# Fused transformer block on one core: the last stacking transfers issued ahead of the second rows of maxima in three slots, and one piece of the context loaded in a later slot

## The reference, cut to what matters

```python
shift_a, scale_a, gate_a, shift_m, scale_m, gate_m = split(silu(c) @ W_mod + b_mod, 6)
q, k, v = split(modulate(ln(x), shift_a, scale_a) @ W_qkv + b_qkv)     # 16 heads of 8
x = x + gate_a * (softmax(q k^T * scale) v @ W_proj + b_proj)          # self-attention
q_c = ln(x) @ W_qc + b_qc
k_c, v_c = split(ln(context) @ W_kvc + b_kvc)
x = x + softmax(q_c k_c^T * scale) v_c @ W_cproj + b_cproj             # cross-attention
x = x + gate_m * (gelu(modulate(ln(x), shift_m, scale_m) @ W_mlp1 + b_mlp1) @ W_mlp2 + b_mlp2)
```

## Time and profile before

| what | value |
|---|---|
| three timed runs | 373.79, 377.98, 378.31 us, median 377.98 us |
| profiled execution | 376.56 us |
| its span in the trace | 374.5 us |
| mean granted TensorE clock | 0.986 of full |
| busy share of PE, DVE, ACT, POOL | 91%, 70%, 72%, 56% |
| TensorE clock by fortieth of the span | 9998889999, then 9 throughout |

### The profile page before, as it was taken

How to read it: one execution, slowest core, us unless ns; L and a number is a source line. 1 busy time by engine, 2 the same in 40 slices (tenths; PEclk the granted TensorE clock), 3 DMA queues, 4 the chain that set the end, 5 groups by cost and what they waited for, 6 DMA issues and landing times. The chain is left out here.

```text
span 374.5 us, 16029 instructions
## 1 busy us (share of the span) xinstructions
PE 339.9 (91%) x5888; PEld 231.6 (62%) x5888; DVE 263.8 (70%) x671; ACT 269.8 (72%) x526; POOL 210.0 (56%) x479
## 2 busy tenths in 40 slices
PE   4677877899899999999999999999798999999996
PEld 3455545577676767777677777767665445554444
DVE  6956658698878889887888979888766754443401
ACT  2336465878888887888879888888776756776673
POOL 6862666777767787777877777777455220112100
PEclk9998889999999999999999999999999999999999
DMA  5744552444344444434344344444324200102001
GB/s 131 155 104 129 140 148 59 95 112 104 86 103 106 100 103 97 101 86 111 93 111 112 74 100 114 100 110 96 89 72 98 68 4 3 30 28 56 28 28 56
DMA packets 65788, 33.13 MB, mean 88 GB/s; under 512 B 8471, under 2 KB 65495, under 8 KB 65751
## 3 DMA queue, kind: packets, MB, share of 16 engines
q1 hardware_dynamic: 63847, 32.36, 35.6%
q10 hardware_dynamic: 1904, 0.27, 0.6%
HBM read 4.83 MB, written 2.10 MB: 18 GB/s over the span
## 5 line engine op out<-in xcount | busy, mean ns | idle before, releaser
L862 DVE TENSOR_REDUCE mx<-wide 128x8 f32<-128x1024 f32 x64 | 78.2, 1221 | 26.4 <-PE wide L1347 26.1
L1080 ACT ACTIVATE p_c<-wide 128x1024 f32<-128x1024 f32 x64 | 65.5, 1023 | 21.5 <-PE wide L1358 20.5
L1080 ACT ACTIVATE p_s<-wide 128x1024 f32<-128x1024 f32 x64 | 65.7, 1026 | 12.5 <-PE wide L1358 12.2
L862 DVE TENSOR_REDUCE mxc<-wide 128x8 f32<-128x616 f32 x64 | 50.7, 792 | 4.4 <-PE wide L1347 4.0
L1369 PE MATMUL ps_o<-p_s,v_m 128*32 128x128 f32 x1024 | 42.4, 284 | 0.2
L1369 PE MATMUL ps_o<-p_c,vc_m 128*32 128x128 f32 x1024 | 41.3, 279 | 0.3 <-ACT p_c L1080 0.3
L1347 PE MATMUL wide<-qk_st 62*128 62x128 bf16 x512 | 26.6, 226 | 11.7 <-DMA qk_st<-qkp 6.6
L1347 PEld LDWEIGHTS wide<-qk_st 62*128 62x128 bf16 x512 | 15.2, 97 | 27.9 <-DVE mx L862 13.0
L1410 PE MATMUL wide<-m_nT,w_sb 128*128 128x512 f32 x64 | 30.1, 600 | 0.2 <-DVE mxc L862 0.2
L1369 PEld LDWEIGHTS ps_o<-p_s,v_m 128*32 128x32 f32 x1024 | 25.0, 111 | 7.5 <-issue 1.9
L1369 PEld LDWEIGHTS ps_o<-p_c,vc_m 128*32 128x32 f32 x1024 | 24.1, 109 | 7.0 <-issue 0.5
(11 more groups left out here) (182 smaller groups left out, 822.9 us busy)
## 6 DMA issues: line engine op xcount, KB each, us to landing
qk_st<-qkp SPq DMA_DIRECT2D x94, 128.0 KB, 2.5
qkc_st<-qkcp SPq DMA_DIRECT2D x90, 128.0 KB, 2.5
out<-m_out SPq DMA_DIRECT2D x7, 256.0 KB, 2.3
xs<-x SPq DMA_DIRECT2D x3, 512.0 KB, 5.1
qk_st<-nmT SPq DMA_DIRECT2D x64, 4.0 KB
qkc_st<-nmcT SPq DMA_DIRECT2D x64, 4.0 KB
ctx_sb<-ctx SPq DMA_DIRECT2D x3, 308.0 KB
w_sb<-L_xcond_W_mlp SPq DMA_DIRECT2D x2, 256.0 KB, 3.0
```

What stands on the lines that cost most here:

```text
L862: nc.vector.reduce_max(mxt[:, b].rearrange("q (x r) -> q r x", r=2)[:, r], src, AX.X, negate=True).then_inc(sems[done], 1)
L1080: nc.scalar.activation(dst[u % 2][:].rearrange("k x q -> k (x q)"), ps_st[:].rearrange("k s x -> k (s x)"), ACT.Exp, scale=SCALE).then_inc ...
```

## The change

In SP's `slot`, a function `rest_first` picks slots 0, 1, 2 and 14. In these the last two stacking transfers of the pair ahead are issued before `max_rows` b = 1. For slot 0 that was so already, so slots 1, 2 and 14 change. `load_c(4)` goes from the end of slot 1 to slot 3, between `max_rows` b = 0 and the stacking transfers that wait for `qk1_set`. No other engine's stream changes.

```diff
+        def rest_first(s, a):
+
+            return a.first(4) and not a.first() or s.left() == 0
...
                     max_rows(qk_st[h.par], 0, nmT, f"m_in{h.par}0")
+                if h and h.first(4) and not h.first(3):
+                    load_c(4)
                 if a:
...
-                if a and a.second():
+                if a and rest_first(s, a):
                     w(sp, "qk2_set", a.n + 1)
                     stack(sp, qk_st[a.par], qkp, f"qk_in{a.par}", SELF_ORDER[2])
                 if h:
                     w(sp, "nmT_set", 2 * h.n + 2)
                     max_rows(qk_st[h.par], 1, nmT, f"m_in{h.par}1")
                 if a:
-                    if not a.first(2):
+                    if not a.first() and not rest_first(s, a):
                         w(sp, "qk2_set", a.n + 1)
                         stack(sp, qk_st[a.par], qkp, f"qk_in{a.par}", SELF_ORDER[2])
-                if h and h.second():
-                    load_c(4)
```

## The result

The changed kernel took 386.32 us in the median of six runs (382.43 to 387.42), the kernel before 378.14 in the same comparison (373.79 to 379.42). The ratio is 1.026, with a 95% interval of 1.021 to 1.031. That is a loss of some 10 us where 4 us (380.5 against 376.56) had been forecast; the measured time lies above the range.

A forecast was written before the change was run, and what follows sets the result against it. PE was taken as nearest to full. Terms -0.6 + 0.3 - 1.4 + 3.5 + 1.6 + 0 = +3.4 us on 376.56 gave 380.0, leaned to 380.5; range 378.5 to 382.5, eight times in ten 376.5 to 385.

The forecast's parts named there:

- Which waits go: Starts of slots 2, 3 and 15: PE's stacking waits gone or small, waits for maxima rows at unit 2 instead.
- How long the new waits are: Unit 2 in slots 1, 2 and 14: PE waits 0.83, 1.18 and 0.94 us for the maxima rows.
- The upper value of 1.1 us given for slot 3: Start of slot 3: loss up to 1.1 us if SP's gap of 0.45 us stays in front of the rows.
- The start of slot 2: PE reaches slot 2 sooner: 0.6 us gained, between 0.35 and 0.8.
- The start of slot 3: PE reaches slot 3 later: 0.3 us lost, up to 1.1.
- The clock of slot 2: The clock's fall behind slot 2's front wait does not come: 1.4 us gained, nothing if it comes all the same.
- Slot 15: Start of slot 15: no change, between 0.3 us gained and 0.6 lost.
- The stall: Slot 3: DVE waits 3.7 us for the context load (2.5 to 5.8), so PE's second cross product stalls 3.5.
- The clock behind the stall: Slot 3, behind DVE's stall: the clock falls, costing 1.6 us.
- The sum: Whole kernel: all terms together 3.4 us slower than the profiled 376.56 us, so 380.0; stated as 380.5.

The follow-up runs named there:

- e5: Kernel before with the new order in slot 14 alone, slots 1 and 2 and the context load as before; ratio 0.9993 to the kernel before.
- e3: Changed kernel with DVE's wait for context piece 4 moved to the end of slot 3; ratio 1.0102 to the kernel before, 3.8 us.
- e1: Kernel before with the new order in slots 1, 2 and 14, context load left at the end of slot 1; ratio 1.0088, 3.3 us slower.
- e2: Kernel before with only the context load moved to slot 3, order as before; ratio 1.0079, 3.0 us slower.
- e10: Changed kernel with the old order in slot 14; ratio 1.0198 to the kernel before, 7.5 us slower.
- e9: The changed kernel itself, unchanged, measured again beside the kernel before on one more chip; ratio 1.0268, 10.1 us slower.
- e6: Kernel before with the new order in slots 1 and 2 alone; ratio 1.0051, 1.9 us slower.
- e12: Kernel before with ACT issuing maxima rows b = 1 in slots 1, 2 and 14 and the context load in slot 2; ratio 0.9941, 2.2 us faster.
- e15: Kernel before with ACT issuing maxima rows b = 1 in slots 1 and 2 and the context load in slot 3; ratio 1.0061, 2.3 us slower.
- e8: Changed kernel with the context load ahead of the first stacking transfer of pair 4 in slot 3; ratio 1.0131 to the kernel before, 4.9 us.
- e14: Changed kernel with the new order kept in slot 2 only; ratio 1.0143 to the kernel before, 5.4 us slower.
- e4: Kernel before with the context load in slot 2, order as before; ratio 0.9989 to the kernel before.

## Why the prediction was wrong, step by step

- **Which waits go.** Right: all three waits for stacking transfers in slots 2, 3 and 15 went in the changed kernel's trace, and waits of unit 2 for `qk_st<-nmT` came in their place, as the prediction had it.
- **How long the new waits are.** Too small. Predicted 0.83, 1.18 and 0.94 us; measured 1.52, 2.46 and 1.59. In slot 1, PE reached unit 2 0.4 us sooner than before (47.68) and the rows took 2.37 us, not the 2.24 of the earlier trace rows. In slot 2 the rows were issued 4.40 us after the first of the five stacking transfers (65.08 less 60.68), not 2.59 and 1.31 (63.97 less 61.38, and the swap): SP's issue of the third took 1.72 us, where it had taken 1.25 before and the others take 0.6. The issue of the rows took 1.57 us, and they landed after 2.92 us. One quiet landing in slot 0 was too little to price a landing behind five stacking transfers. The upper value of 1.1 us given for slot 3 does not follow from the gap of 0.45 us that it names (0.26 and 0.45 are 0.7).
- **The start of slot 2.** Predicted 0.6 us gained, a term that failed: slot 1 became 0.5 us longer over all traces. The gain rested on the removal of a wait of 1.64 us, and that wait was one draw. It stood in three of five traces of the old order, where slot 1 took 16.3 to 16.7 us; in the other two it was 0.44 and 0.43 us, and slot 1 took 15.3 and 15.0. The eight traces of the new order lie between and above, at 15.8 to 17.1.
- **The start of slot 3.** Predicted 0.3 us lost, and this is a term that failed: with the new order slot 2 is 2.3 us longer over all traces. The wait itself grew by 1.5 us (2.46 less the 0.92 that it replaces), and the clock falls behind it, which I had not counted there.
- **The clock of slot 2.** Predicted 1.4 us gained; another term that failed. The fall that I read in the earlier trace rows is not a feature of the order. With the same order up to there, slot 2 was 17.54 us in one trace and 15.38 in another (e5). I took one draw for a cost that could be removed. In the changed kernel the clock fell sooner, behind slot 1's wait. The net gain of 1.7 us put on slots 1 and 2 (0.6, less 0.3, and 1.4) became a loss of 0.5 us in slot 1 and 2.3 in slot 2.
- **Slot 15.** Predicted nothing; 0.7 us over the traces, not resolved in time by itself (e5).
- **The stall.** Right in mechanism and size: 4.0 us on DVE and 3.88 on PE, predicted 3.7 and 3.5, inside 2.5 to 5.8. e3, with the wait moved, shows that it is the wait. The fit of the Trainium skill (DMA: Bandwidth & Descriptors, "Anatomy of one DMA — SWDGE (gpsimd) path") would have made it too short: it is stated for transfers that GpSimd issues, its 2.7 us are an estimate, and this load, issued by SP, landed after 3.6 to 5.9 us.
- **The clock behind the stall.** Predicted 1.6 us. In the changed kernel's own trace it was 6 us at half clock, and slot 3 grew by 6.2 us in all, 2.3 us more than PE's wait. Over eight traces slot 3 grew by 4.3 us, and PE's wait was 3.4 in the mean (3.2 to 3.9), so 0.9 is left for the clock. So 1.6 us was too much as a mean and too little for this trace; the spread is what I lacked.
- **The sum.** The forecast of 3.4 us was -1.7 for the order and 5.1 for the load. Measured alone: +3.3 and +3.0. The order has the wrong sign, and that is 5.0 us of error; the load alone was overrated by 2.1 us. Of the 6.7 us missed (10.1 less 3.4) these make 2.9. The rest, 3.8 us (10.1 less 3.3 and 3.0), is in neither part alone. The three intervals together leave this some 3 us uncertain.

**What stays open.** The last 3.8 us. By the lengths of slots there is less of it: the new order's 0.5, 2.3 and 0.7 us make 3.5, about e1's 3.3, but the load makes slot 3 4.3 us longer, where e2's time grew by only 3.0 (1.5 to 4.4). With the load, slot 3 is 20.7 us long behind a slot 2 of the new order (five traces) and 20.2 otherwise (three).

The clock looks like an answer and is not shown to be one. The mean granted clock of the runs was 0.982 to 0.986 for the kernel before, 0.979 for e1, 0.986 for e2, and 0.966 and 0.955 for the changed kernel (0.959 for e10). But this mean is no measure of time lost. Call 1 less the granted clock, times the length of a stretch, its missing clock. In e9's trace 17 us are missing over the whole span, and 9.8 of them lie before slot 1. There the clock is at half from 18 us on, and PE is busy hardly longer than in the kernel before. One window of each (the kernel before, then e9):

```profile
18.00:33.00 15.00, 10.06 (x111) 6.87 (x111) 9.98 (x22) 7.05 (x13) 8.54 (x19) 0.99 0.41 94
```

```profile
18.00:33.00 15.00, 10.28 (x109) 7.15 (x109) 10.60 (x22) 6.70 (x13) 8.21 (x19) 0.50 0.41 93
```

Slot 1 begins on the ruler at 36.1 us in e9 and at 35.3 to 36.4 in the kernel before, e2, e5 and e6, which had full clock there or nearly. The trace of e12, the fastest of all, is at half clock in that window too. And of the runs of the kernel before that enter the ratios of e1 to e15, 48 had a mean clock of 0.99 or more and took 376.6 us in the mean, and 29 had 0.96 to 0.975 and took 376.4. From slot 1 on, 4.1 us of clock are missing in the kernel before, 7.9 in e1, 3.5 in e2, 10.3 in the changed kernel's first trace and 7.3 in e9's; 7.3 is also what e1 and e2 make added up (7.9 and 3.5, less 4.1). So one trace has more than the sum of the parts and the other has not. No run here sets the clock by itself. The last section names another candidate, and the cause of the last 3.8 us stays open.

## What to carry to other kernels

A swap of two groups on an issuing queue removes one wait and makes another: price the group that is moved back by the slack of its own consumer, and where that slack is under the issue time of what passes it (here 0.1 to 0.5 us against 1.3), look for a second queue instead; giving the small group to an engine with a gap removed both waits. Before a load is moved later, find the first instruction that waits for its semaphore, not the first that reads its bytes: the wait for piece 4 stood nine pairs ahead of its use. And a drop of the clock, or a late landing, seen in one trace is not a cost that an edit can be credited with: look at it in a second execution first. The mean clock of a run does not say what it lost: look where the clock was low, and whether the engine was late there.

## What the runs showed of the hardware

- The same 308 KB load took 3.6 (e2), 4.3 (the changed kernel) and 5.9 us (e8) from issue to its consumer's start. In the two longer cases more stacking transfers stood just ahead of it, and a packet of instructions (of the kind described next) was under way until 79.2 and 79.7 us, after its issue; which of the two counts was not tried. Issuing it 2.3 us sooner brought it in 0.7 us sooner (e8).
- The last stacking transfer of slot 1 took 4.0 us to land in the kernel before, where the median is 2.5, though it was issued on time. The context load was not the cause (e2). While that transfer was in flight, one packet of another queue passed, of instructions (queue, packets, MB, share; window 49 to 50 us):

```profile
q8 instruction: 1, 0.02, 6.6%
```

  Such a packet is 16 KB, and this one took 1.06 us. It began 1.89 us after the issue of the transfer and ended at 2.95. Of the transfer's 128 packets, 125 had ended by 2.08 us, as all of them had in e5 and e14, and the last three ended at 3.06 to 3.27. In e2 and e4 four packets were late in the same way, just behind the end of a packet of instructions. In the other 14 traces, whatever the order, none began in the first 2.1 us, and the transfer landed after 2.4 to 2.7.
- The same packets go along with two more delays. In each of the 17 traces SP's longest issue in slot 2 (1.2 to 1.9 us, where 0.6 is usual) begins within 0.2 us of one. And in all eight traces in which PE waits 36 us behind the start of slot 15, one began 0.6 to 2.4 us behind the issue of the first of six transfers of `qkcp` there; of the nine without the wait, two had that. An edit that delays a slot changes which transfers these packets meet. That is a rival cause for the part of the loss that neither edit gives alone, and for some of the noise. No run here moves the packets by themselves, so it is argued, not shown.
- A stall of 3.2 to 3.9 us on PE was followed by anything from hardly a fall of the clock (e8) to 6 us at half (the changed kernel). The Trainium skill (TensorE: Matmul & The Clock Gate, "Part 1: The HAM clock gate") says that the number of products that a kernel begins with at half clock varies from run to run of the same kernel. The traces here show the like for falls in the middle of a kernel: with the same order up to there, slot 2 had 1.7 us of clock missing in the kernel before and none in e5.
